# A four-layer graph network on one core: bf16 turning of the one-hots in layer 0's first sum pass, and stored one-hots with paired powers in layer 2

## The reference, cut to what matters

```python
# layer 0 (run for l = 0, 1): an attention over edges, then a second sum back to the nodes
a = leaky_relu(xt[row] @ att[:H] + et[col] @ att[H:])
ex = exp(a - segment_max(a, col)[col]);  alpha = ex / segment_sum(ex, col)[col]
eout = segment_sum((Binv[col] * stoich * alpha)[:, None] * xt[row], col)   # pass "a" of the kernel
nout = segment_sum((Dinv[row] * stoich * alpha)[:, None] * eout[col], row) # pass "b" (l = 0) or "f" (l = 1)

# layer 2: a gated message with a layernorm inside
h    = gelu(se @ W1a + de @ W1b + b1);  h = gelu(h @ W2 + b2)              # pass "d" of the kernel
msg  = layernorm(h @ W3 + b3, ln_g, ln_b)
gate = sigmoid(gelu(se @ Wg1a + de @ Wg1b + bg1) @ Wg2 + bg2)
upd  = segment_sum(gate * msg, edge_dst);  out = upd @ W_out + b_out
```

## Time and profile before

| | |
|---|---|
| Median of 3 runs | 13288.62 us (13284.19 to 13300.03) |
| The profiled execution | 13297.17 us, its span 13295.4 us |
| Busy share of the span | PE 64%, DVE 63%, ACT 35%, POOL 68% |
| Mean granted clock of TensorE | 0.711 of full speed |
| Passes that the change touches | b from 3527.9 us, d up to about 10475 us of the span |

### The profile page before, as it was taken

One profiled execution on the slowest core, in us unless ns is written; L12 is line 12 of the kernel. 1 busy time (PEld: TensorE's weight loads), 2 busy tenths in 40 slices (PEclk: granted clock), 3 DMA queues, 4 the chain that ended last, 5 costly groups with the idle time before them and its releaser, 6 DMA issues. The chain is left out here.

```text
span 13295.4 us, 183873 instructions
## 1 busy us (share of the span) xinstructions
PE 8533.5 (64%) x47919; PEld 6720.4 (51%) x47919; DVE 8392.4 (63%) x30342; ACT 4699.2 (35%) x13637; POOL 9082.4 (68%) x9335
## 2 busy tenths in 40 slices
PE   3310173777788867776555355558999677767776
PEld 0000131777677757776444245547777545444554
DVE  9960031888644457776444522238999688878887
ACT  0000162444333324443000111125666456645664
POOL 5777777777666647776777377746888477747775
PEclk9999965777655557776555577679999865665656
DMA  0000152222545552224555444443333444454445
GB/s 17 2 2 18 25 209 84 54 55 54 74 118 118 118 86 57 53 53 59 132 132 132 62 131 131 133 70 103 88 88 88 79 128 133 135 101 132 135 132 106
DMA packets 634173, 1206.33 MB, mean 91 GB/s; under 512 B 208682, under 2 KB 319944, under 8 KB 632136
## 3 DMA queue, kind: packets, MB, share of 16 engines
q0 software_dynamic: 305600, 572.24, 23.4%
q1 hardware_dynamic: 327560, 622.33, 14.1%
HBM read 960.69 MB, written 233.16 MB: 90 GB/s over the span
## 5 line engine op out<-in xcount | busy, mean ns | idle before, releaser
L426 POOL DMA_INDIRECT WK<-tab,IDX x4640 | 4475.3, 965 | 1896.2 <-issue 1309.4
L1221 POOL DMA_INDIRECT B<-tab,IDX x1856 | 1764.4, 951 | 901.7 <-issue 503.4
L749 PE MATMUL PS<-WK 128*128 128x129 f32 x5568 | 1166.6, 374 | 571.8 <-ACT WK L967 492.5
L749 PEld LDWEIGHTS PS<-WK 128*128 128x128 f32 x5568 | 993.1, 268 | 778.0 <-ACT WK L967 544.2
L1240 DVE TENSOR_REDUCE WK<-PS 128x4 f32<-128x1024 f32 x928 | 1131.5, 1221 | 226.5 <-PE PS L1366 224.5
L1351 ACT ACTIVATE B<-B 128x33 f32<-128x33 f32 x5568 | 1211.1, 308 | 7.9
L426 POOL DMA_INDIRECT H<-tab,IDX x928 | 899.9, 970 | 347.0 <-issue 257.3
L336 POOL DMA_INDIRECT recd<-B x831 | 818.7, 985 | 338.9 <-issue 271.4
L668 ACT ACTIVATE WK<-WK 128x128 f32<-128x128 f32 x1856 | 592.9, 390 | 1272.3 <-DMA WK<-tab,IDX 1251.3
L336 POOL DMA_INDIRECT recd<-REC,B x831 | 830.5, 999 | 272.9 <-issue 272.9
L1399 PEld LDWEIGHTS PS<-B,H 128*128 128x128 f32 x3712 | 817.8, 329 | 277.7 <-issue 277.7
(11 more groups left out here) (381 smaller groups left out, 19893.5 us busy)
## 6 DMA issues: line engine op xcount, KB each, us to landing
H<-onehots SPq DMA_DIRECT2D x232, 768.0 KB
onehots<-B SPq DMA_DIRECT2D x232, 384.0 KB
B<-onehots SPq DMA_DIRECT2D x232, 384.0 KB
WK<-onehots SPq DMA_DIRECT2D x232, 384.0 KB
WK<-tab,IDX POOLq DMA_INDIRECT x4640
onehots<-WK SPq DMA_DIRECT2D x232, 256.0 KB
onehots<-B SPq DMA_DIRECT2D x232, 128.0 KB
B<-tab,IDX POOLq DMA_INDIRECT x1856
```

What stands on the lines that cost most here:

```text
L426: po.indirect_dma_start(out=G[:, g % n, k, :], out_offset=None, in_=table, in_offset=bass.IndirectOffsetOnAxis(ap=IDX[:, idx, t:t + 1], ax ...
L749: mm = pe.matmul(AG(r, k // 2), OH[:, r, k, :], R[:, r % 2, k, 0:129], start=k % 2 == 0, stop=k % 2 == 1)
L1221: po.indirect_dma_start(out=eG[:, g % 4, k, :], out_offset=None, in_=tab[TW3], in_offset=bass.IndirectOffsetOnAxis(ap=IDX[:, o, t:t + 1], ...
```

## The change

Pass b (layer 0, l = 0):

- ACT's float32 copy of the turned one-hot (L763 with its buffer bOT and signal `ot`) is gone. The `sv` fetch reads the bf16 copy bTBt instead, with three bf16 matmuls for each tile from a split table (BP), twelve for a group in place of four float32 ones. The table is split into three parts before the pass (`l0_mid_ve`) in place of one copy.
- PE turns the one-hot with four bf16 matmuls instead of float32 transposes: the stationary operand is the upper half of each float32 of the one-hot (bOHb, a view with a step of two bf16 elements) and the moving one is a bf16 identity.
- ACT's copy now waits also for the fetch of four groups earlier, and PE's turning for ACT's copy of two groups earlier.

Pass d (layer 2):

- DVE makes no one-hots (L743) and PE turns none (L757). SP streams both stored forms back, the turned bf16 one (128 KB) in turn j for group j and the float32 one (256 KB) for group j-5 (`d_sp`). ACT widens the turned one from SBUF to float32, where before it copied the turned one out of PSUM.
- POOL computes the power for two groups at once, in every second turn.
- DVE's use of the power, ACT's scaled rows, PE's sum and DVE's add each move one turn later (lags 7, 7, 8, 9 become 8, 8, 9, 10), and small rings grow from two to four.

```diff
-    "b": dict(oh=1, pt=1, ot=1, sv=1, ...
+    "b": dict(oh=1, pt=1, sv=1, ...
-KEPT = {"a": 0, "b": 48, "f": 16, "c": 16, "d": 0, "e": 32}
+KEPT = {"a": 0, "b": 48, "f": 16, "c": 16, "d": 16, "e": 32}
...
+        bOHb = bOH.rearrange("p r k n -> p (r k n)").bitcast(BF16).rearrange("p (r k n h) -> p r k n h", r=8, k=4, h=2)[:, :, :, :, 1]
+        BP = B2[:, 0:76].bitcast(BF16)
...  (b_ac)
                     ac.wait_ge(S.pt, at.pt + g + 1)
+                    ac.wait_ge(S.sv, at.sv + g - 3)
                     ac.activation(bTBt[r % 4], PS[:, r % 2, :], ACT.Copy).then_inc(s_kt, 1)
-                    turned_ac(ac, at, g, r, bOT, r % 2)
...  (b_pe)
-                    pe.wait_ge(S.ot, at.ot + g + 1)
+                    pe.wait_ge(s_kt, CREDIT + NG + g + 1)
                     pe.wait_ge(S.p2, at.p2 + g - 1)
                     for k in range(4):
-                        mm = pe.matmul(PS[:, 2 + r % 2, k:k + 1], bOT[:, r % 2, 128 * k:128 * k + 128],
-                                       B2[:, bass.ds(v[k // 2], 1)], start=True, stop=True)
+                        for i in range(3):
+                            mm = pe.matmul(PS[:, 2 + r % 2, k:k + 1], bTBt[r % 4][:, 128 * k:128 * k + 128],
+                                           BP[:, bass.ds(v[k // 2] * 3 + i, 1)], start=i == 0, stop=i == 2)
                     mm.then_inc(S.sv, 1)
                 if f := turn(j, u, 1):
-                    turn_pe(pe, at, *f, bOH, f[1] % 2, 2)
+                    g, r = f
+                    pe.wait_ge(S.oh, at.oh + g + 1)
+                    pe.wait_ge(s_kt, CREDIT + NG + g - 1)
+                    for k in range(4):
+                        mm = pe.matmul(PS[:, r % 2, 128 * k:128 * k + 128], bOHb[:, r, k, :], identb, start=True, stop=True)
+                    mm.then_inc(S.pt, 1)
...  (d_po)
-                if j >= 6:
+                if j >= 7 and j % 2 == 1:
                     g = j - 6
+                    c = slice(g % 4 - 1, g % 4 + 1)
                     po.wait_ge(S.mv, at.mv + g + 1)
-                    po.wait_ge(S.r, at.r + g - 1)
-                    po.tensor_tensor(dRS[:, g % 2, :], dVE[:, g % 2, :], dPW, ALU.pow).then_inc(S.rs, 1)
+                    po.wait_ge(S.gw, at.gw + g - 3)
+                    po.tensor_tensor(dRS[:, c, :], dVE[:, c, :], dPW, ALU.pow).then_inc(S.rs, 2)
...
+        def d_sp(sp, p):
+            at, ring = raised_before(p)
+            for j in range(NG + 5):
+                if j < NG:
+                    sp.wait_ge(S.ot, at.ot + j - 3)
+                    sp.dma_start(dSTt[:, j % 4, :], oht[0][j, :, 0:256].bitcast(BF16)).then_inc(s_kd[j % 4], 16)
+                if j >= 5:
+                    g = j - 5
+                    sp.wait_ge(S.ag, at.ag + g - 3)
+                    sp.dma_start(dOH[:, g % 4, :, :].rearrange("p k n -> p (k n)"),
+                                 oht[0][g, :, 256:768]).then_inc(s_st[g % 4], 16)
...  (d_ve)
-                    ve.wait_ge(S.rs, at.rs + gw + 1)
+                    ve.wait_ge(S.rs, at.rs + gw + 2 - rw % 2)
...
-                if f:
-                    onehot_ve(ve, at, 0, *f, dOH)
...  (d_ac)
                 if f := turn(j, u, 1):
-                    turned_ac(ac, at, *f, dOT, 0)
-                if f := turn(j, u, 7):
+                    g, r = f
+                    streamed(ac, p, g, r)
+                    ac.wait_ge(S.sv, at.sv + g - 1)
+                    ac.activation(dOT[:, r % 2, :], dSTt[:, r % 4, :], ACT.Copy).then_inc(S.ot, 1)
+                if f := turn(j, u, 8):
...  (d_pe)
-                if f := turn(j, u, 1):
-                    turn_pe(pe, at, *f, dOH, 0, 1)
-                if f := turn(j, u, 8):
+                if f := turn(j, u, 9):
+                    landed_oh(pe, *f)
                     sum_pe(pe, at, *f, dOH, dR, AGd, 1)
```

More of the change, by code:

```diff
@@ L748, in sum_pe @@
             for k in range(4):
-                mm = pe.matmul(AG(r, k // 2), OH[:, r, k, :], R[:, r % 2, k, 0:129], start=k % 2 == 0, stop=k % 2 == 1)
+                mm = pe.matmul(AG(r, k // 2), OH[:, r % OH.shape[1], k, :], R[:, r % 2, k, 0:129], start=k % 2 == 0,
+                               stop=k % 2 == 1)
             mm.then_inc(S.ag, 1)
@@ L911, in body @@
                 if f := turn(j, u, 4):
-                    sum_pe(pe, at, f[0], f[1] % 4, fSTo, bR, AGb, 2)
+                    sum_pe(pe, at, *f, fSTo, bR, AGb, 2)
                 if f := turn(j, u, 1):
@@ L976, in body @@
                 if f := turn(j, u, 3):
-                    sum_pe(pe, at, f[0], f[1] % 4, cSTo, cR, AGb, 2)
+                    sum_pe(pe, at, *f, cSTo, cR, AGb, 2)
                 if f := turn(j, u, 1):
@@ L994, in build @@
         fd = [[WK[:, 0:8704], 0]]
[L995 to L998, removed]
+        dOT, dR, dH2, dZ3 = room(fd, 2, 512), room(fd, 2, 4, 133), room(fd, 512), room(fd, 4, 512)
+        dSTt = room(fd, 4, 256).rearrange("p r c -> p (r c)").bitcast(BF16).rearrange("p (r c) -> p r c", r=4)
+        dOH = room(fd, 4, 4, 128)
+        dBN, dMV = room(fd, 2, 4, 6), room(fd, 4, 4, 2)
+        dVE, dRS, dGT = (room(fd, 4, 4) for _ in range(3))
+        dTH, dGW, dNM, dGL = (room(fd, 2, 4) for _ in range(4))
+        dPW = room(fd, 2, 4)
         hf, xf = flat(H[:, :, :]), flat(X[:, :, :])
@@ L1023, in d_po, with landed_oh @@
                     rows_po(po, p, 0, tab[256], dG, j)
+        def landed_oh(eng, g, r):
+            base = 16 * NGR
+            eng.wait_ge(s_st[r % 4], base + 16 * (g // 4 + 1) if isinstance(g, int) else (g - r % 4) * 4 + (base + 16))
+        def d_sp(sp, p):
[9 more added lines that the diff above has]
+                                 oht[0][g, :, 256:768]).then_inc(s_st[g % 4], 16)
         def d_ve(ve, p):
@@ L1028, in body @@
             def body(j, u):
-                z, w, l, f = turn(j, u, 6), turn(j, u, 7), turn(j, u, 5), turn(j, u, 0)
-                if x := turn(j, u, 9):
+                z, w, l = turn(j, u, 6), turn(j, u, 8), turn(j, u, 5)
+                if x := turn(j, u, 10):
                     add_ve(ve, at, 0, *x, AGd)
@@ L1043, in body @@
                     ve.wait_ge(S.p3, at.p3 + gz + 1)
-                    ve.wait_ge(S.rs, at.rs + gz - 1)
-                    ve.wait_ge(S.r, at.r + gz - 1)
-                    ve.tensor_tensor(by128(dZ3[:, qz, :]), by128(PS[:, 5, :]),
+                    ve.wait_ge(S.r, at.r + gz - 3)
+                    ve.tensor_tensor(by128(dZ3[:, rz % 4, :]), by128(PS[:, 5, :]),
                                      b3b.unsqueeze(1).broadcast_to([128, 4, 128]), ALU.add).then_inc(S.z3, 1)
@@ L1079, in body @@
                     ve.wait_ge(S.th, at.th + gz + 1)
-                    ve.tensor_scalar(dGT[:, qz, :], dTH[:, qz, :], 0.5, 0.5, ALU.mult, ALU.add)
+                    ve.tensor_scalar(dGT[:, rz % 4, :], dTH[:, qz, :], 0.5, 0.5, ALU.mult, ALU.add)
                     for k in range(4):
-                        i = ve.bn_aggr(dMV[:, qz, k, :], dBN[:, qz, k, :])
+                        i = ve.bn_aggr(dMV[:, rz % 4, k, :], dBN[:, qz, k, :])
                     i.then_inc(S.mm, 1)
@@ L1086, in body @@
                     ve.wait_ge(S.mm, at.mm + gz + 1)
-                    ve.tensor_scalar(dVE[:, qz, :], dMV[:, qz, :, 1], EPS, None, ALU.add).then_inc(S.mv, 1)
-                if f:
-                    onehot_ve(ve, at, 0, *f, dOH)
+                    ve.wait_ge(S.rs, at.rs + gz - 2 - rz % 2)
+                    ve.tensor_scalar(dVE[:, rz % 4, :], dMV[:, rz % 4, :, 1], EPS, None, ALU.add).then_inc(S.mv, 1)
             for i in range(NGR - 4, NGR):
@@ L1093, in d_ve @@
             meet(ve)
-            sweep(9, body)
+            sweep(10, body)
         def d_ac(ac, p):
@@ L1125, in body @@
                     for k in range(4):
-                        i = ac.activation(dR[:, q, k, 0:128], dZ3[:, q, 128 * k:128 * k + 128], ACT.Identity,
+                        i = ac.activation(dR[:, q, k, 0:128], dZ3[:, r % 4, 128 * k:128 * k + 128], ACT.Identity,
                                           bias=dNM[:, q, k:k + 1], scale=dGW[:, q, k:k + 1])
@@ L1129, in d_ac @@
             meet(ac)
-            sweep(7, body)
+            sweep(8, body)
         def d_pe(pe, p):
@@ L1169, in d_pe @@
             meet(pe)
-            sweep(8, body)
+            sweep(9, body)
         eMX = WK[:, 2048:2048 + 36 * (NO + 1)]
@@ L2264, in _ @@
             meet(sp)
+            d_sp(sp, 5)
             meet(sp)
```

22 lines of the change are left out of this document (9 added, 13 removed).

## The result

The changed kernel took 13198.59 us (median of 4 runs, 13189.04 to 13208.54), the kernel before beside it 13292.42 us (13284.19 to 13300.03). The ratio is 0.993, with a 95% interval of 0.9912 to 0.9947: faster by 94 us, where 194 were forecast and where 13055 to 13175 was the range. The profiled execution took 13189.04 us, 108 us less than the one before.

A forecast was written before the change was run, and what follows sets the result against it. The prediction took a PE-ACT ring to bound pass b and POOL, closely followed by a ring, pass d. Gains of 156 (b) and 39 (d), less 1 for the table split, made 194 off 13288.6: 13095 us, range 13055 to 13175.

The forecast's parts named there:

- b's ring: Pass b: PE and ACT wait on each other in a loop; 5.81 us a group, forecast to become 4.59.
- The turning: Pass b: four bf16 matmuls on PE turn the one-hot in 0.55 us, 0.54 less than before.
- the fetch: Pass b: twelve bf16 one-column matmuls take 0.89 us in place of 1.57, 0.68 less.
- The new waits and the stores: Pass b: waits for earlier groups cost nothing; stores might be late next, but their 4.5 us fit.
- rival 1: Pass b stops short of POOL's pace, period 5.3 to 5.6 us; b gains 60 to 130 us; chance 0.13.
- POOL takes over: Pass b: with the ring at 4.59 to 5.13 us, POOL's gathers set the pace and the remaining gain is lost.
- I price the pass by f from end to end: Pass b would take f's time, 1195.7 us in place of 1351.6: 156 us less.
- 140 to 170: Pass b's gain in us: low end for two close limits, high end at POOL's bare 5.00 a group.
- The 170: Pass b: upper gain in us, at POOL's bare 5.00 us a group in place of f's 5.18.
- 39: Pass d's net gain in us: 45 from POOL's paired power, less 6 for one more turn of lag.
- The power of 128x8: Pass d: POOL's power for two groups takes 1.68 us, interpolated from measured powers, giving 5.85 us a turn.
- an estimate of about 1.05: Pass d: by the page's rule the paired power takes about 1.05 us, and the pass gains 54 instead of 45.

The follow-up runs named there:

- the third kernel: Changed kernel with pass b's fetch in one PSUM bank and b's four weights and the one-hot's row in PSUM: 13108.66 us, ratio 0.9874.
- c (added instruction): Changed kernel plus one unused DVE addition per group of pass c: 17122.75 us (1.0228) with two SBUF operands, 17087.4 (1.0215) with one in PSUM.
- the kernel before with the same edit: Kernel before with weights of a, f and d and a's one-hot row moved to PSUM, b untouched: 13228.93 us, ratio 0.9945.

## Why the prediction was wrong

**b's ring: right.** The turning has the length that I gave it (0.59 us for 0.55), and the fetch puts 0.37 us between its start and the turning's in place of 0.89, a busy time that I had set against a way from start to start; this error fell in slack and cost the forecast nothing, and the ring has slack: from bits to bits it is now 0.53 + 1.88 + 0.37 + 0.59 + 0.10 + 0.63 = 4.10 us (medians between 4000 and 4600 us, and the 0.10 before ACT's copy as it was before the change), which leaves 1.3 of the 5.41. The new waits and the stores cost nothing; rival 1 had the right gain for b (60 to 130), but none of its causes (longer turning, register steps, stores) happened.

**"POOL takes over": right. "I price the pass by f from end to end": the step that failed.** I took a pass's pace over from another pass, and with it a gather's 1.25 us from start to start as a fixed pace. It is one only where DVE does nothing that holds it. The price of b from its own rows: POOL starts four gathers in each 5.0 us, DVE has two instructions with two SBUF operands in a group, each holds a gather that starts in its first 0.57 us, and for 0.28 us in the mean. That is 4 x 2 x 0.57 / 5.0 = 0.91 held gathers a group, times 0.28 is 0.26, times 232 is 59 us. Measured are 68. This sum takes the starts as spread evenly over the period, and where the two engines keep step it is off: for f it gives 30 us (measured 12 before, 16 after), for each pass a 55 (measured 18 and 45). In f only the weighing is of that kind, and f's own long gathers (26 before) were already in the 5.18 that I took; b has twice the instructions and made 173. The term was -156 and came out at -99; with the operands in PSUM on both sides it is -166, within the 140 to 170 that I gave. The 170 had no working in the prediction (0.18 us on 232 groups, from 5.18 to 5.00, would put 42 on top of 156), so that it met the 170 us between the first and last weighings of before and of the third kernel is luck.

**d: right in kind, 8 to 13 us short** (26 us pass to pass in the first trace, 28 to 31 in the others with the whole change of d, of 39). The power of 128x8 takes 1.674 us (1.68 forecast). The rule of the GPSIMD Engine Reference in the Trainium skill (section 3.1), from which I had put an estimate of about 1.05 beside it, does not hold for a power here: four more columns cost 0.63 us. The turn is 5.877 us in place of 5.85, which is 6 us over the pass, and d's product made 21 long gathers. With the weights in PSUM the turn is 5.862. The few us that are left were not traced.

**What was not in the sum.** The second a and f took 6 and 14 us more. The gather of 0.955 us makes 10 in each; in f 4 more are collisions (45 long in place of 26), and in the second a the collisions were 2 us less. So of the 194 us, 57 were lost in b to collisions, 13 in d, and 20 in two passes that I had held to be untouched. That leaves 104 of the 108 us between the two profiled executions; the rest is in the start and the other passes, up to 7 us each, of both signs. The 94 us between the medians are another 14 less, and that is spread: the prediction put the median 8.6 us below the profiled execution, and it came 9.6 above it.

**The range** was too narrow at its upper end. The collisions in b alone would not have left it (13095 + 57 = 13152, under 13175), nor would those and d's 13 (13165); the 20 us of two passes that I put at nothing without a reason took it out, to 13185, and the median's spread did the rest. The largest part is still b's: every bound assumed that a POOL that never waits runs at the pace of its rows. The rows of before had the sign: f's gathers have a mean of 0.956 us between 6500 and 7200 us, where single ones in c take 0.94, and 26 of f's are over 1.1.

**The rule that bears on this.** The rows above show that a gather is held by a DVE instruction that reads two SBUF operands, and not by one that reads a single one. The page SBUF — State Buffer of the Trainium skill (Who interferes with whom) says that DVE with two SBUF inputs contends with a GpSimd instruction that reads SBUF, and the trace agrees: the powers of d, which read SBUF, are held beside L1089 (1.20 us in place of 1.04) and not when its weights are in PSUM. That a gather is held by its reading of its 128 offsets is a reading that fits, and is not shown by itself. The same section tells of a probe in which `tensor_tensor` did not seem to stall a DMA, and infers why from the ports that descriptor writing needs; there the runs differ: the gather is held by up to 0.5 us (1.45 in place of 0.944). Weighed against the change, this page would have given a rival at 13095 + 59 = 13154 by the sum above (an estimate, and a high one, since f's own 12 us of lengthened gathers are in 13095 already).

## What to carry to other kernels

When an engine takes over as the bound, do not carry its pace over from another pass: look at what the other engines do while it works, and whether a resource is shared. For GpSimd's indirect gathers beside DVE, count the wide DVE instructions with two SBUF operands: in this kernel a first estimate of what each costs per group is the number of gathers times 0.57 us over the period, times 0.28 us. It was near in b (59 for 68 us) and up to three times too high in a and f, so read the starts from the trace where you can. Putting the smaller operand (four weights, a row of constants) in PSUM took all of it away at no cost to DVE (0.69 us either way), and was worth more here on the changed kernel (145 us, 13175.89 to 13030.93 on one chip) than the change under study (94 to 109 us); on the kernel before, with b left as it was, it was worth 77.

## What the runs showed that was not expected

- A gather that starts 0.05 to 0.57 us into a two-SBUF instruction of 0.69 us ends 0.817 us after it (spread 3 ns), with the same figure in b, in c (added instruction) and within 0.01 us in d and in the changed kernel's f; of those that start in the first 0.05 us some are held and some are not; if it starts later, or beside an instruction with an operand in PSUM, it takes 0.944.
- A gather's base length has two values, 0.944 and 0.955 us, that hold for a whole pass; which one the second a and f have went with the paired power in a later pass, and the cause is not found.
- Streaming more (d's DMA share from 0.31 to 0.52) cost the gathers nothing: with the collisions away, d's turn with streams and unpaired powers is 6.06 us, and so it is on the same chip in the kernel before with the same edit.
